# Causal heads: the turning of the next head's maxima moves two scores later in PE's order

## The reference, cut to what matters

```python
Q, K, V = x @ qw, x @ kw, x @ vw          # 2048 x 16 heads x 8
Q, K = rope(Q, freq), rope(K, freq)
score = einsum('bhqd,bhkd->bhqk', Q, K) / sqrt(8)
score = score - 1e10 * (1 - tril(ones))
weights = softmax(score - max(score, -1), -1)
attn = einsum('bhqk,bhkd->bhqd', weights, V)
return merged(attn) @ ow
```

## Time and profile before

| what | us |
|---|---|
| median of 3 runs | 1954.57 (1953.61 to 1955.54) |
| profiled execution, its own time | 1957.02 |
| its span, first to last instruction | 1955.2 |
| mean granted TensorE clock | 0.928 |
| PE busy | 1706.5 |
| DVE busy | 1409.8 |
| ACT busy | 1158.1 |

### The profile page before, as it was taken

The page is one execution under the profiler, slowest core; times in us unless marked ns, Lnnn a source line. Parts: engine busy times, 40 slices in busy tenths (PEclk is TensorE's granted clock), DMA queues, the critical chain, the costliest instruction groups (busy, mean ns, idle before and its releaser), DMA issues. The chain is left out here.

```text
span 1955.2 us, 44123 instructions
## 1 busy us (share of the span) xinstructions
PE 1706.5 (87%) x17561; PEld 805.5 (41%) x17561; DVE 1409.8 (72%) x2622; ACT 1158.1 (59%) x2294; POOL 311.3 (16%) x522
## 2 busy tenths in 40 slices
PE   4699999999999995789997798892599999999966
PEld 2222222222222223434445445881335555555456
DVE  5889999999999934755556417747688888888525
ACT  3278888888888893332222344451227777777734
POOL 0001000000001000000000436442103223211123
PEclk9789999999999997899997898996669999999988
DMA  4112111221111021052223379852401111111032
GB/s 136 40 48 65 61 50 50 79 66 55 50 51 44 17 49 68 1 97 90 90 74 142 97 223 341 247 162 95 146 21 37 35 29 32 32 32 31 7 89 81
DMA packets 78037, 154.52 MB, mean 79 GB/s; under 512 B 18684, under 2 KB 35964, under 8 KB 74136
## 3 DMA queue, kind: packets, MB, share of 16 engines
q1 hardware_dynamic: 63152, 121.57, 20.2%
q0 software_dynamic: 14384, 29.29, 4.8%
q10 hardware_dynamic: 296, 0.85, 0.1%
HBM read 102.23 MB, written 48.89 MB: 77 GB/s over the span
## 5 line engine op out<-in xcount | busy, mean ns | idle before, releaser
L817 ACT ACTIVATE heads_probs<-heads_pS 128x512 f32<-128x512 f32 (+3 forms) x1664 | 850.7, 574 | 170.3 <-PE heads_pS L683 155.6
L683 PE MATMUL heads_pS<-heads_qs,heads_ks 75*32 75x512 bf16 (+3 forms) x6656 | 623.3, 372 | 17.9 <-ACT heads_probs L817 16.4
L841 DVE TENSOR_REDUCE heads_run_max<-heads_pM 128x1 f32<-128x1024 f32 x512 | 592.9, 1218 | 56.9 <-PE heads_pM L705 55.6
L745 PE MATMUL heads_pO<-heads_probs,heads_vh 128*32 128x512 f32 (+2 forms) x3328 | 437.5, 570 | 1.4 <-ACT heads_probs L817 1.4
L683 PEld LDWEIGHTS heads_pS<-heads_qs,heads_ks 75*32 75x32 bf16 x6656 | 187.1, 95 | 304.4 <-ACT heads_probs L817 143.8
L683 PE MATMUL heads_pM<-heads_ks,heads_qs 72*32 72x512 bf16 (+3 forms) x2560 | 277.2, 367 | 12.7 <-DMA heads_qs<-k_parts_dram 10.2
L852 DVE TENSOR_REDUCE heads_run_max<-heads_pM 128x1 f32<-128x512 f32 x384 | 246.9, 684 | 37.0 <-PE heads_pM L683 35.0
L705 PE MATMUL heads_pM<-heads_ks,heads_qs 64*128 64x512 bf16 x512 | 185.5, 396 | 17.5 <-DVE heads_run_max L841 16.2
L705 PE MATMUL heads_pM<-heads_kd,heads_qd 64*128 64x512 bf16 x512 | 185.6, 397 | 0.0
L849 DVE CUSTOM_DVE_ANT_0 heads_masked_out<-heads_pM,heads_mask_end 128x128 bf16<-128x128 f32 (+3 forms) x256 | 121.9, 486 | 34.1 <-PE heads_pM L683 30.9
L683 PEld LDWEIGHTS heads_pM<-heads_ks,heads_qs 72*32 72x32 bf16 x2560 | 97.7, 97 | 111.0 <-DVE heads_run_max L852 38.2
(11 more groups left out here) (375 smaller groups left out, 2046.4 us busy)
## 6 DMA issues: line engine op xcount, KB each, us to landing
top_weights<-k_comb_dram SPq DMA_DIRECT2D x128, 128.0 KB, 3.0
second_w<-in_L_W_dram SPq DMA_DIRECT2D x12, 1024.0 KB, 9.5
k_hid_slots_dram<-k_zeros SPq DMA_DIRECT2D x8, 1152.0 KB, 4.8
k_h_slots_dram<-second_work SPq DMA_DIRECT2D x48, 192.0 KB, 2.6
second_work<-k_hid_slots_dram SPq DMA_DIRECT2D x48, 192.0 KB, 4.1
k_parts_dram<-proj_part SPq DMA_DIRECT2D x12, 512.0 KB, 3.9
heads_qs<-k_parts_dram SPq DMA_DIRECT2D x64, 96.0 KB
heads_ks<-k_parts_dram SPq DMA_DIRECT2D x60, 96.0 KB
```

The costliest lines, as they stand in the source:

```text
L683: mm = pe.matmul(out[cols, :], still[:, cols], moving, start=start, stop=stop)
L745: mm = pe.matmul(pO[k * 32:k * 32 + VW, int(second), o:BLK], vh[c][:, t, :], probs[u % 2][:, k * BLK + o:(k + 1) * BLK], start=first_chunk ...
L817: act.activation(probs[u % 2][:, k * BLK + c0 - b * BLK:(k + 1) * BLK], pS[:, slot, 0:c1 - c0], ACT.Exp)\
L841: dve.reduce_max(run_max[:, i, blocks[0][0] // 2:blocks[0][0] // 2 + 1], both.rearrange("p k c -> p (k c)"), AX.X).then_inc(taken, 2)
```

## The change

`TURN_AT` gets two added where the heads are causal: 33 in place of 31. Layer 0 keeps its value. In PE's order the turning then stands behind score 31, a filling, score 32 and a filling, ahead of score 33. ACT's copy stands behind the exps of chunks 31 and 32. The chunks 31 and 32 are one event earlier in the ring. SP's wait moves with it. The copy of a head's sums stays where it is, on ACT.

```diff
     TURN_UNIT = min(u for u in range(NU) if upto[u] + LEAD >= ITEMS + SLACK)
-    TURN_AT = first_chunk[TURN_UNIT + 1] + RING
+    TURN_AT = first_chunk[TURN_UNIT + 1] + RING + (2 if causal else 0)
     EVENTS = NC + 1
```

## The result

The change is slower, by 0.2%: median 1961.17 us (1956.04 to 1965.96, 20 runs) against 1955.34 (1951.08 to 1961.48, 20 runs), ratio 1.0022, 95% interval 1.0014 to 1.0031. Forecast were 1951.4 us and a range of 1948.2 to 1956.5. The profiled execution has a span of 1959.3 us, 4.1 over that of before.

The account below looks back on a forecast made before the run. TensorE (PE) was taken to bound the kernel, busy 87% of the span and 48.3 of 50 us in the causal heads. 14 x 0.23 = 3.2 us off the median 1954.57 gave 1951.4 us, range 1948.2 to 1956.5.

Parts of the forecast that it names:

- The gap at the turning: PE's turning waits for POOL's split of the maxima; 0.57 us lost per head, at most 0.42 winnable.
- the ring (a, d): Turning later in PE's order ends POOL's wait; s33 and s34 then wait for exps 31 and 32, costing 0.19 us.
- Won: 0.23 us a head: Sum 7 at 1576.98 instead of 1577.21 in each causal head, carried to the next head's first score.
- The rows (b, c): ACT's row copy and SP's three row DMAs go 0.72 us later; claimed to cost nothing in scatter heads.
- The place of the need: Next head's first score needs all three rows landed by 1580.32, 2.4 us after the third issue.
- the 0.2 us of margin: In scatter heads the third row was to land about 1580.1, in time by 0.2 for the next first score.
- today only the third row's landing is late: Said of the kernel before, within the rival where all three rows queue behind the scatter.
- The prediction's own sign of failure: Forecast fails if third rows land over 2.4 us after their issue as a rule.
- The slower side: All three rows queue behind the scatter, first score 1.05 us late in eight heads: 1959.8 us; chance 0.10.
- Landing goes with the issue: Each third row keeps its present delay, 3.3 us together, eating the win: 1954.6 us, no change; chance 0.13.
- The faster rival: ACT doesn't hold the scores back, so up to 0.42 us a head is won: 6.3 us, 1948.3 us; chance 0.17.
- DVE takes it back: DVE's unmasked maxima pace the head, so PE arrives early and waits for banks: 1954.6 us; chance 0.08.

Follow-up runs that it names:

- the repetitions: The unedited change run twice more against the kernel before: ratios 1.0019 (1962.66 us against 1957.99) and 1.0042.
- the kernel with late rows: Kernel before, turning unmoved, SP's three row DMAs held back by two exps (1.1 us): 1973.61 us against 1958.32; ratio 1.0010 on the slower chip.
- the pair with the scatter moved: Second token scatter issued at the first one's place, ahead of the split: with the change ratio 0.9990, in the kernel before 0.9994.

## Why the prediction was wrong

**The gap at the turning and the ring (a, d): right.** Sum 7 was forecast 2.87 us behind sum 6 and is at 2.87; exp 31 at 1.29, the copy at 2.27 and s34 at 2.43 were measured at 1.29, 2.26 and 2.42. The period was to be 26.4 to 26.5 and is 26.47. "Won: 0.23 us a head" holds in undisturbed heads, with 0.2 left over the whole head. POOL's wait and ACT's idleness in front of the copy are gone, as forecast, and DVE did not take it back: PE's wait for DVE's unmasked maxima fell from 24.0 to 19.2 us.

**The rows (b, c): wrong, and here the forecast failed.** The step was: the lateness "belongs to the scatter, which does not move ... and the third row should land at the later of 1580.1 and 1577.91 + 1.7 = 1579.6: in time by 0.2". The place of the need (2.4 us behind the third issue) was right. But the row's lateness has a second source that I had not looked up in the trace: packets of the instruction queue. In the kernel before the third row of head 7 landed in 1.88 us, at 1632.87, and a 16 KB fetch of 2.7 us began at 1633.29, 5.57 us behind the reduction. The change sent the same row 0.7 us later in the head, and the fetch began 0.5 us earlier in it, at 5.07 (5.05 and 5.20 in the repetitions), so one packet of the row stood behind the fetch, 3.2 us long. The same collision makes heads 4 and 7 of both repetitions and heads 1, 4 and 7 of the kernel with late rows. No run moves a fetch by itself: its part rests on these packet times. A landing distribution read from rows at their present place said nothing about the place they were moved to. I had noted that two slow rows had no scatter beside them and gave "something else delayed them" no further look.

Two smaller slips stand beside it. The scatter is issued 2.80 us behind the reduction in both kernels, but in head 1 it lands after 3.65 us instead of 2.69, in head 5 after 3.49 instead of 3.25, and the third row 0.3 to 0.4 behind it, so the 0.2 us of margin was not there. And "today only the third row's landing is late" misread the trace: head 3 already had a second row of 2.90 us. The prediction's own sign of failure came true: 8 first scores wait for rows, and 7 of 15 third rows took over 2.4 us.

**The price of a wait: mis-sized.** I counted a late landing one to one. After a stop of 2.71 us the clock fell to the 1.2 GHz level for 7 us and added 2.5 us in head 7; in heads 4 and 7 of the repetitions it fell for 3.4 to 6.8 us after stops of 2.9 to 3.0 us. It does not follow each such stop (2.72 us without a fall in the kernel with rows held back). In the profiled execution, 14 x 0.2 = 2.8 us were won; against them stood 377.9 - 14 x 26.45 = 7.6 us, of which 5.4 are head 7, 1.8 together heads 1, 3, 4 and 6, and the rest is spread; before had 373.8 - 14 x 26.65 = 0.7 us of such excess.

**The rivals.** The slower side was given as all three rows queueing behind the scatter, 1.05 us in each of eight heads, chance 0.10. The place and the sign were right, the mechanism was not: most of the loss lies in one or two heads, the rest are tenths, and in none does the second row land after the third. That its 1959.8 us lies near the measured 1961.2 is luck. "Landing goes with the issue" missed because the delays didn't travel with a row: heads 9 and 12 had third rows of 3.06 and 3.31 us before and 2.65 and 2.43 in the change, head 7 went from 1.88 to 5.31. The faster rival and "DVE takes it back" are out by the period of 26.47. The share of the scatter is shown by the pair with the scatter moved: 377.9 (381.4 on the same chip) against 372.8 us, where before goes from 373.8 to 373.2.

The rule from the Trainium skill, "DMA: Bandwidth & Descriptors", section "Queues, rings and completion order", was weighed in the prediction as if it only excused the later issue. It speaks of every earlier write of a DMA engine across its queues; that a packet of the instruction queue stands in the way of a row's last packet is shown by the rows above. What waits there is the data packet itself, which goes at 1636.40, and not the increment alone. The page's advice in its section "Rules for kernel authors", to issue early and wait late, came true in this case, at 15 us for 1.1 us of delay.

Left open: why a fetch takes 3.2 us beside a scatter, when most take 0.9 to 1.4, why SP's issue stalls for 1.1 us in head 3, and the idle time of PE in the scatter heads on the slower chip.

## What to carry to other kernels

When an instruction moves, its DMAs move with it: measure how much room the last of them has, and judge it by the worst that is in flight at the new place, instruction fetches too, not by the median at the old one. Move a waiting instruction only as far as its wait needs (one score here, not two), and win room for the DMA by issuing it from a second queue. A rare wait of 3 us on PE can cost nearly twice its length, when the clock falls behind it.

## What was unexpected of the hardware

- Fetches of instructions show as packets of 16 KB beside the kernel's own DMAs, and hold back single packets of them. Behind one of 3.2 us a 4 KB transfer took 5.3 us instead of 1.7.
- Such a fetch took 2.5 to 3.5 us beside a scatter and 0.9 to 1.5 us at the same place with the scatter moved away.
- A stop of PE of 2.71 us was followed by 7 us at a granted clock of 0.51, which cost 2.5 us more; one of 2.72 us in another kernel was followed by 1.00 and cost 2.8 us in all.
- Three DMAs by SP take 1.82 us to issue; with the third given to ACT the periods were 26.43 (26.44 to 26.48 without), so ACT's issue cost nothing measurable there.
- One chip ran the same kernel in 2024 us instead of 1956 to 1958, and in the kernel with rows held back the heads with scatters took 28.4 us there, 1.7 longer than those without. Comparisons across chips would have misled.
